# Preln decoder block on one core: banks of the sums and side steps alternate, sums turned by DMA

## What is computed

```python
x = x + _L0_attn_ref(_layernorm(x), ...)            # one head, width 128
x = x + _L0_xattn_ref(_layernorm(x), ctx_768, ...)  # 16 heads of 64, 1601 keys
x = x + _L0_ffn_ref(_layernorm(x), ...)             # 31 chosen tokens per batch

# _L0_xattn_ref
sim = jnp.einsum('bhid,bhjd->bhij', q, k) * SCALE
attn = jax.nn.softmax(sim, axis=-1)
out = jnp.einsum('bhij,bhjd->bhid', attn, v)
return out.transpose(0, 2, 1, 3).reshape(B, Nq, HEADS * DIM_HEAD) @ Wo + bo
```

## Time and profile before

| | us |
|---|---|
| median of three runs | 2164.53 (2164.51 to 2168.09) |
| span of the profiled execution | 2169.9 |
| TensorE matmul busy | 2103.3, 97% |
| GpSimd busy | 1933.6, 89% |
| ScalarE busy | 1832.2, 84% |
| VectorE busy | 1736.7, 80% |

### The profile page before, as it was taken

The page is one execution under the profiler, slowest core; times in us unless marked ns, Lnnn a source line. Parts: engine busy times, 40 slices in busy tenths (PEclk is TensorE's granted clock), DMA queues, the critical chain, the costliest instruction groups (busy, mean ns, idle before and its releaser), DMA issues.

```text
span 2169.9 us, 58374 instructions
## 1 busy us (share of the span) xinstructions
PE 2103.3 (97%) x22087; PEld 1544.3 (71%) x22087; DVE 1736.7 (80%) x4158; ACT 1832.2 (84%) x3124; POOL 1933.6 (89%) x1127
## 2 busy tenths in 40 slices
PE   8999999999999999999999999999999999999998
PEld 4677777777777777777777777777777777777665
DVE  7778878787887888879687797878878788886764
ACT  6898898989888888998888888898878888888872
POOL 3899999999999899999899998998989999899991
PEclk9999999999999999999999999999999999999999
DMA  3110000000000000000000000000000000000000
GB/s 73 42 38 13 2 13 2 2 13 2 13 2 2 13 2 13 2 13 2 11 13 2 13 2 2 14 2 13 2 11 13 2 13 2 2 2 2 2 11 11
DMA packets 17366, 22.10 MB, mean 10 GB/s; under 512 B 5872, under 2 KB 14976, under 8 KB 17088
## 3 DMA queue, kind: packets, MB, share of 16 engines
q1 hardware_dynamic: 15984, 18.17, 3.0%
q10 hardware_dynamic: 1104, 0.20, 0.1%
HBM read 16.14 MB, written 2.10 MB: 8 GB/s over the span
## 4 chain that ended last, share of the span: by engine, by line
PE 76%; DVE 11%; issue 5%; ACT 5%; POOL 2%; DMA 0%; SPq 0%; DVEq 0%; ACTq 0%; POOLq 0%
PE PS L573 14%; PE PS L613 13%; PE PS L574 13%; PE PS L590 11%; PE PS L592 10%; PE PS L636 4%; DVE EH L1091 4%; PE PS L646 2%; PE PS L623 2%; DVE over L1114 2%; POOL EL L1566 2%; ACT PF L897 2%; PE PS L657 1%; ACT over L919 1%; DVE junk L1359 1%
## 5 line engine op out<-in xcount | busy, mean ns | idle before, releaser
L1566 POOL TENSOR_TENSOR EL<-PF,EH 124x1024 f16<-124x1024 f32 x828 | 1761.7, 2153 | 144.0 <-DVE EH L1091 69.4
L897 ACT ACTIVATE PF<-PS 124x512 f32<-124x512 f32 x1664 | 972.6, 602 | 203.7 <-PE PS L574 190.1
L590 PE MATMUL PS<-Ch,EH 123*128 123x97 f16 (+1 forms) x6656 | 765.8, 207 | 22.9 <-POOL EL L1566 22.2
L592 PE MATMUL PS<-Cl,EL 123*128 123x97 f16 (+1 forms) x6656 | 762.3, 207 | 0.0
L1091 DVE TENSOR_SCALAR_CACHE_REDUCE EH<-PF 124x1024 f16<-124x1024 f32 x621 | 746.1, 1209 | 18.1 <-ACT PF L897 16.9
L590 PEld LDWEIGHTS PS<-Ch,EH 123*128 123x128 f16 (+1 forms) x6656 | 609.1, 98 | 181.5 <-issue 62.7
L1114 DVE CUSTOM_DVE_ANT_1 over<-over,PS 128x806 f32<-128x806 f32 x512 | 506.6, 989 | 284.7 <-ACT over L919 142.8
L592 PEld LDWEIGHTS PS<-Cl,EL 123*128 123x128 f16 (+1 forms) x6656 | 597.8, 98 | 168.2 <-issue 1.9
L573 PE MATMUL PS<-AH,ChT 97*124 97x512 f16 x1664 | 646.6, 389 | 6.5 <-ACT PF L897 5.8
L574 PE MATMUL PS<-AL,ClT 96*124 96x512 f16 x1664 | 633.7, 381 | 0.0
L919 ACT ACTIVATE over<-PS 128x806 f32<-128x806 f32 x512 | 433.4, 846 | 28.6 <-PE PS L613 8.6
(11 more groups left out here) (248 smaller groups left out, 1766.9 us busy)
## 6 DMA issues: line engine op xcount, KB each, us to landing
Cf<-in_ctx SPq DMA_DIRECT2D x16, 546.0 KB
X<-in_x SPq DMA_DIRECT2D x16, 128.0 KB, 2.4
out_x<-X SPq DMA_DIRECT2D x16, 128.0 KB, 1.7
msk<-in_attention_mask SPq DMA_DIRECT2D x4, 256.0 KB, 4.3
AH<-mh SPq DMA_DIRECT2D x63, 2.0 KB
Cf<-in_ctx SPq DMA_DIRECT2D x16, 53.6 KB
xWqT<-in_xWqT SPq DMA_DIRECT2D x2, 256.0 KB, 6.5
xWo<-in_xWo SPq DMA_DIRECT2D x2, 256.0 KB, 4.3
```

The source lines that it names most:

```text
L590: pe.matmul(PS[:, 6, u0:u0 + DC + 1], EH[0:kr, r, qs], Ch[j][0:kr, t, :], start=(t == 0 and q == 0), stop=False, skip_group_check=True)
L592: m = pe.matmul(PS[:, 6, u0:u0 + DC + 1], EL[0:kr, r, qs], Cl[j][0:kr, t, :], start=False, stop=(t == KT - 1), skip_group_check=True)
L897: act.activation(PF[:, n % PRING, :], PS[0:KP, 4 + n % 2, :], ACT.Exp).then_inc(sg("ex"), 1)
L1566: pool.tensor_tensor(EL[:, r - 1:r + 1, :], PF[:, f - 1:f + 1, :], EH[:, r - 1:r + 1, :], ALU.subtract).then_inc(sg("lo_pool"), 1)
```

## The change

1. The sums of pair x lie in bank 6 + x % 2. A side step takes the other one of banks 6 and 7, that of the pair before (`bank_at`). It waits until the sums held there have been read out (semaphore `ul`), and the first `av` of the next pair waits for the last side step that held its bank (`given_up`). Every `av` stands exactly eight tiles behind its `st`.
2. The copy to U is gone. VectorE multiplies the sums in PSUM by their reciprocals in place (`norm`), ScalarE rounds them to a float16 high part, and VectorE subtracts for the low part (`u_split`, both into UHL).
3. The 384 TensorE transposes of Un and their copies are gone. The DMA queue of SyncE turns UHL into UT (`turn_u`, one transfer of 128 x 1536 float16, 384 KB, per quad, 64 in all), in an order of its own (`orders["sp"]`).
4. M is split once, in batch 0, into MH and ML (`m_max`, `mtop`, `msplit`). A `proj` is 12 float16 matmuls of 128 columns. Its scale is applied when VectorE adds to X.
5. The places of side steps and the table LATER are other ones. `sa_s` stands at 13 (before 12), `sel_row` at 37 (35), `ctx_t` at 54, 57, 65, 67 (55, 60, 62, 64), `sa_t` and `sa_qk` at 3 and 5 (5 and 7), `proj` at places 3 modulo 13, the chosen tokens' steps at 24, 76, 81, 89, 97 (24, 82, 84, 87, 94).
6. `sel_rank` on VectorE forms rank in two instructions and keep with an accumulator output.
7. At the end 24 filler matmuls stand before the last `proj`, in place of 4 and 1.

```diff
-SA_PLACES = (5, 7, 10, 12, 30, 32, 56)
-SEL_PLACE = 35
-TURN_PLACES = (55, 60, 62, 64)
-SIGMA_PLACE = 72
+SA_PLACES = (3, 5, 11, 13, 30, 32, 36, 41, 56)
+SA_PLACES_0 = (14, 16, 20, 25, 39, 41, 45, 50, 65)
+SEL_PLACE = 37
+TURN_PLACES = (54, 57, 65, 67)
+SIGMA_PLACE = 71
+M_PLACE = 36
+SPLIT_LATER, TURN_LATER, PROJ_LATER = 1, 4, 9
+CHOSEN_PLACES = (24, 76, 81, 89, 97)
...
         late = n - AV_LAG
-        if late >= 1 and late % KT == 1:
-            put(n, "av", late - 1)
-        if late >= 0 and late % KT:
+        if late >= 0:
             put(n, "av", late)
...
+        if done >= 0 and done % KT == 0 and done // KT < B * HP - 1:
+            put(n, "norm", done // KT)
+        if done >= 0 and done % KT == SPLIT_LATER:
+            put(n, "u_split", done // KT)
+        for later, kind in ((TURN_LATER, "turn_u"), (PROJ_LATER, "proj")):
+            if done >= 0 and done % (2 * KT) == KT + later:
+                quad = done // (2 * KT)
+                put(n, kind, quad // QD, quad % QD)
...
+            if s.kind == "av" and s.a[0] % KT == 0:
+                pair = s.a[0] // KT
+                sums_before[pair] = holder.get(6 + pair % 2)
+                holder[6 + pair % 2] = ("sums", pair)
...
+            return (sg("ul"), holder[1] + 1) if holder[0] == "sums" else left(holder)
...
                 elif k == "proj":
                     b, qd = s.a
+                    w.wait_ge(sg("ut"), 16 * i)
+                    kb = bank_free(s)
+                    w.wait_ge(sg("m_lo"), 1)
+                    for t in range(T):
                         for c in range(QC):
-                            m = pe.matmul(PS[:, kb, t * D:(t + 1) * D], UT[:, t, c, :], M[:, qd * QC + c, :],
-                                          start=(c == 0), stop=(c == QC - 1))
+                            for part, of in enumerate((MH, ML)):
+                                m = pe.matmul(PS[:, kb, t * D:(t + 1) * D], UT[:, (part * T + t) * QC + c, :],
+                                              of[:, qd * QC + c, :], start=(c == 0 and part == 0),
+                                              stop=(c == QC - 1 and part == 1))
...
+                elif k == "u_split":
+                    x, = s.a
+                    b, qd = x // HP, x % HP // 2
+                    w.wait_ge(sg("un"), x + 1)
+                    w.wait_ge(sg("ut"), 16 * max(0, b * QD + qd - 1))
+                    act.activation(
+                        UHL[qd % 2][:, 0, :, 2 * (x % 2):2 * (x % 2) + 2, :].rearrange("p t h c -> p h t c"),
+                        sums_bank(x)[:, :, 0:DC].rearrange("p (h t) c -> p h t c", t=T),
+                        ACT.Copy, scale=KEEP).then_inc(sg("uh"), 1)
...
+                    w.wait_ge(sg("av"), (x + 1) * KT)
+                    dve.reciprocal(rden_u[:, x % 2, :], sums[:, :, DC]).then_inc(sg("u_r"), 1)
+                    w.wait_ge(sg("u_r"), x + 1)
+                    dve.tensor_tensor(sums[:, :, 0:DC], sums[:, :, 0:DC],
+                                      rden_u[:, x % 2, :].rearrange("p (q o) -> p q o", o=1).to_broadcast([P, 4, DC]),
+                                      ALU.mult).then_inc(sg("un"), 1)
...
+                    w.wait_ge(sg("uh"), x + 1)
+                    dve.tensor_tensor(UHL[qd % 2][:, 1, :, hs, :].rearrange("p t h c -> p h t c"),
+                                      sums_bank(x)[:, :, 0:DC].rearrange("p (h t) c -> p h t c", t=T),
+                                      UHL[qd % 2][:, 0, :, hs, :].rearrange("p t h c -> p h t c"),
+                                      ALU.subtract).then_inc(sg("ul"), 1)
...
+                elif k == "turn_u":
+                    b, qd = s.a
+                    w.wait_ge(sg("ul"), b * HP + 2 * qd + 2)
+                    w.wait_ge(sg("pj_mm"), b * QD + qd)
+                    sp.dma_start(UT[:, :, :], UHL[qd % 2][:, :, :, :, :].rearrange("p w t h c -> p (w t h c)"),
+                                 transpose=True).then_inc(sg("ut"), 16)
```

235 lines of the change are left out of this document (111 added, 124 removed).

## The result

The changed kernel takes 2464.8 us (median of four runs, 2461.1 to 2468.9) against 2165.5 for the kernel before: 13.75% slower, ratio 1.1375 with a 95% interval of 1.1356 to 1.1394. The forecast was 2195 in 2095 to 2270. The side was right, the size was not: 299 us came where 30 were summed.

What follows compares the result with a forecast made beforehand. TensorE, busy 97%, was taken as the bound, three engines close beside it. Terms -90.8 - 36 + 56 + 39 + 35 + 21 + 4 + 2 = +30 us on 2169.9 gave 2200, as median 2195; range 2095 to 2270.

Steps and rivals of the forecast that it cites:

- a): Self-attention scores, then q at place 14, waiting for exponentials behind VectorE's maximum: 4.0 us in 14 batches, +56 us.
- b): sa_f, then ctx_t at place 57, waiting for X2T behind the context's maximum: 13 batches, +39 us.
- c): q, then ctx_t at places 54 and 67, waiting for AL: 1.17 us twice in 15 batches, +35 us.
- its sign of being wrong: Profile after: forecast wrong if waits a) to c) sum to under 60 us, or TensorE waits for UT before proj.
- a wait added there time lost: TensorE: each added wait was taken as time lost, since the existing waits are small.
- TensorE's 90.8 us: TensorE: turns removed, 44.8 us; projections of 90.2 us replaced by float16 ones of 44.2; sum -90.8 us.
- Small waits gone, -36: TensorE: the 22.2 us of EL waits and a third of 42.5 us on exponentials go, -36 us.
- d): Seven lesser handovers per batch, such as proj and placemax: 0.2 us each, bound 0 to 126, +21 us.
- Transfer late: Rival: the transposing DMA transfer lands late, some 1300 us more, or 700 at twice the slow row; chance 0.06.
- ScalarE takes over: Rival: ScalarE's high part waits for VectorE, delaying exponentials; 64 us over 128 pairs, 2260; within the 0.50 for summed waits.
- Faster: Rival: the waits do not add up, as VectorE has no backlog; -70 us, median 2095; chance 0.36.
- no change: Rival: savings and waits cancel within 0.2%, 2160 to 2169 us; chance 0.08.

Runs made afterwards that it cites:

- e9: Kernel before with the float16 proj alone, TensorE's transposes kept: 2175.3 us, ratio 1.0030.
- e15: e8 with sel_rank on VectorE at place 74 in place of 59: 2298.2 us, ratio 1.0583.
- e16: e15 with the high and low part of the sums (both u_split) two tiles later: 2313.7 us, ratio 1.0654.
- e3: Changed kernel with the maximum of the self-attention scores two tiles earlier on VectorE: 2431.1 us, ratio 1.1223.
- e1: Changed kernel with X2T moved ahead of the context's maximum on VectorE: 2414.6 us, ratio 1.1147.
- e4: Changed kernel with filler matmuls on TensorE before ctx_t at 54 and 57 and q at 14: 2398.1 us, ratio 1.1071.
- e2: Changed kernel with sel_rank eight tiles later on VectorE, place 58 for 50: 2431.9 us, ratio 1.1227.
- e17: e15 with sel_rank five tiles earlier on VectorE, place 69 for 74: 2251.7 us, ratio 1.0383.
- e12: e9 with sel_rank four tiles later and ln0 one tile later on VectorE: 2230.8 us, ratio 1.0292.
- e6: Changed kernel with ScalarE's u_split shifted by one, which left the order of instructions the same: 2458.8 us, ratio 1.1341.
- e8: Changed kernel with score maximum and X2T earlier, sel_rank nine later, side-step places relaxed and proj two places later: 2309.1 us, ratio 1.0650.

## Why the forecast was right in its side and wrong in its size

The three waits that the forecast named, a to c, were put at 130 us and measured 141; its sign of being wrong, under 60, did not show, and TensorE waited for UT for 1.4 us in the whole run. That the sum of the three is so near is in part luck, since a was 20 us too high and c 30 too low. The steps that failed are the following. A wait was priced at its length ("a wait added there time lost"), with nothing for the clock behind it: at least 67 us. The small waits were counted as falling by 36 us: those of `st` for its exponential rose by 52. Handovers not in the list at all cost 43. And in c the duration was taken from a row with too little in VectorE's line: 30.

**TensorE's 90.8 us: right.** A `proj` takes 0.67 us where 0.69 was taken; the turns are gone. That a TensorE instruction taken away is "mostly time gained" was too strong: e9 saves 46 us and gains none.

**Small waits gone, -36: half wrong.** EL's wait on TensorE fell from 22.2 to 7.0 us as assumed. The exponentials' did not shrink by a third: the idle time before `st` rose from 5.8 to 57.4 us, and on the weight loads from 42.5 to 107.1. The step saw ScalarE do less and did not see it stand for VectorE's product (74.4 us), which in e15's order causes two thirds of such waits, as e16 shows.

**a) 56 us for `q` at place 14: measured 36**, 2.6 us each for 4.0. e3 takes 21.5 of it away and gains 34. Mechanism right, the size between the two bounds.

**b) 39 us for `ctx_t` at 57: measured 39.8**, 50 with its clock (e1).

**c) 35 us for 54 and 67: measured 64.6.** The second was well sized, 12.8 us. The first was not, 51.8 us in 15 batches, 3.5 each for the 1.17 taken and beyond the bound of 1.5. What failed is the duration, taken from a row in which VectorE had only the end of a `fold` in line: AH was ready at 884.52 and AL started at 885.20.

```profile
883.84 0.68 ACT L933 ACTIVATE AH<-PS,qscale 96x512 f16<-96x512 f32 x1
...
884.28 0.99 DVE L1114 CUSTOM_DVE_ANT_1 over<-over,PS 128x806 f32<-128x806 f32 x1
```

After the change those 0.7 us are 2.8. `sel_rank`, whose additions wait for GpSimd, stands four places ahead of that handover (50 for 54, before 48 for 55), with a rounding and a `fold` behind it. The bound "at most 1.5" took no account of what VectorE has in line.

**d) 21 us for seven lesser ones: measured 31.** `proj` then `placemax` cost 19.2 us, and not evenly but in one of the four per batch; `sel_row` then `q` 6.0, the two behind a `ctx_t` 2.7 each. What the list lacked cost more, 43 us: 13.5 for an `av` behind the addition of the self-attention to X, 9.0 for a `proj` behind AL, 8.2 for an `av` behind kT, 7.4 for a `q` behind the chosen tokens, 5.0 for a `sa_t` behind AL.

**The missing term: the clock.** The sum priced a wait at its length. e4 shows at least 67 us on top, by TensorE's 1.2 GHz level behind long waits. It does not fall behind each: in the 13 tiles with the wait of 2.6 us at place 14 the granted clock was 1.00 in four of batches 2 to 13 and 0.84 or 0.92 in the other eight (in e3, with that wait at 1.1 us, 1.00 in all twelve), and in those with the waits at 54 and 57 it was 0.93 or lower in all twelve. The prediction had no row of it, since the kernel before has next to no wait of that length (0.997).

**The account.** The waits of the changed kernel named above come to 251 us more than before, against 246 us more idle time. TensorE's busy time rose by 51 us where 91 were taken away, 142 in all; of these e4 explains 91, and some 50 stay without a run. (The 142 is rough, since the 91 taken away is counted from start to start.)

**The rivals.** *Transfer late:* falls. It took 3.7 us from issue to landing, and not 7 or 10 (the row after, of the DMA issues, us last):

```profile
UT<-UHL SPq DMA_TRANSPOSE x64, 3.7
```

The estimate of 15.7 us from the Trainium skill's one-block figure (VectorE: DVE Perf Modes, "The three transpose paths") does not carry over to twelve blocks in one transfer. *ScalarE takes over:* it was a part of the answer with too small a price and chance. ScalarE waited 74.4 us for the product, up to 3.4 each, and exponentials stand behind it. e16 takes that wait away, and the time does not fall, as side steps then wait for the bank of the sums. *Faster* and *no change:* fall. The upper end of the range does not follow from its own words either: d) at half its bound (+42) and ScalarE's part (+64) on 2195 are 2301, not 2270. And the range had no room for a term that was not in it.

**What stays open.** The experiments do not add up one by one: e1, e2 and e3 give 117 us apart and 69 with each other, as waits stand in for one another. e17 is still 83 us above the kernel before; its largest idle times are `st` behind its exponential at 37 and 38 (1.6 us per batch for the two), `av` behind an addition to X at 34 (1.2) and `q` behind the exponentials at 14 (1.1), and how much of it would go was not tried. Its 13 tiles from place 33 still take 19.4 us, before 15.8, the largest rest of any stretch. What the alternation of banks costs by itself, without the split on VectorE, was not run.

## What to carry to other kernels

A handover is priced by what its clearing engine has in line at that moment, and not by the duration of the clearing instruction: list what stands between the producer and the clearing instruction in the new order, take each at its longest and not its mean, and add what it costs TensorE's clock if the wait is some us long. A long item that is free on a side engine while there are three tiles of slack costs its whole length and more once the slack is gone, so that moving one step (e12: 55 us, e17: 46 us) can matter as much as half of the 91 us of work taken from the engine that is 97% busy. Compare the new order of instructions with the old before running a shift: e6 changed none. And an arithmetic saving on that engine is worth testing alone first (e9: nothing).

## What the runs showed of the hardware that was not expected

- Behind a wait of 3.6 us TensorE ran 4.8 us at a granted clock of 0.50, a `st` matmul 0.63 us for 0.38. Filler matmuls inside three waits per batch brought the mean clock from 0.949 to 0.991 and the time down by 67 us (e4).
- A VectorE instruction of 0.35 us (X<-X,keep) took 2.20 us with an EL of GpSimd under way and ended 0.15 us behind it; KD of 0.57 us took 1.88 in e8. Which instruction meets the EL changes with every shift.
- One transposing transfer of 128 x 1536 float16, 384 KB, lands 3.7 us after its issue, faster than its size scaled from plain loads, and holds SyncE's queue for 1.45 us.
